# Expert gates fetched with the tokens, and the first expert layer's 64-channel parts paired on row halves

## What is computed

```python
xn2 = _layernorm(x, norm2_w, norm2_b).reshape(-1, C)         # 1152 x 192
logits = xn2 @ w_gate                                        # 8 experts
top_vals, top_idx = jax.lax.top_k(logits, 2)
gates = jax.nn.softmax(top_vals, axis=-1)
gates_full = zeros((T, E)).at[arange(T)[:, None], top_idx].add(gates)
# for every expert (w1 192x768, w2 768x192), with its column g of gates_full:
h = jax.nn.gelu(xn2 @ w1 + bb1, approximate=False)
acc = acc + g[:, None] * (h @ w2 + bb2)
return x + acc
```

## Time and profile before

| | us |
|---|---|
| median of 3 runs | 381.36 (380.62 to 381.72) |
| the profiled execution's own time | 382.74 |
| its span in the profile | 380.7 |
| PE busy / PEld / DVE / ACT / POOL | 319.8 / 285.3 / 229.8 / 167.8 / 83.5 |
| routing begins (DVE L1097) | 252.16 |
| first scatter issued | 282.62 |
| last scatter issued | 375.18 |

### The profile page before, as it was taken

The page is one execution under the profiler, slowest core; times in us unless marked ns, Lnnn a source line. Parts: engine busy times, 40 slices in busy tenths (PEclk is TensorE's granted clock), DMA queues, the critical chain, the costliest instruction groups (busy, mean ns, idle before and its releaser), DMA issues.

```text
span 380.7 us, 6780 instructions
## 1 busy us (share of the span) xinstructions
PE 319.8 (84%) x2358; PEld 285.3 (75%) x2358; DVE 229.8 (60%) x557; ACT 167.8 (44%) x399; POOL 83.5 (22%) x79
## 2 busy tenths in 40 slices
PE   7959740870597998999999989887999999999990
PEld 4948630560477787897898767786899999999990
DVE  1626999999998965416468478787333333333330
ACT  0053610524441519778796988314333333333320
POOL 9310002001000011101001000102225455556532
PEclk9989985796598999999999999997599999999997
DMA  7970000000000019691383133040102222222322
GB/s 262 317 223 3 0 0 0 0 2 0 1 2 1 0 46 282 196 270 55 106 245 86 37 85 125 25 116 13 43 10 38 38 45 41 44 43 42 47 29 23
DMA packets 20590, 28.01 MB, mean 74 GB/s; under 512 B 3459, under 2 KB 15475, under 8 KB 20555
## 3 DMA queue, kind: packets, MB, share of 16 engines
q1 hardware_dynamic: 16666, 23.52, 20.8%
q0 software_dynamic: 3888, 4.03, 7.2%
HBM read 22.77 MB, written 4.77 MB: 72 GB/s over the span
## 4 chain that ended last, share of the span: by engine, by line
PE 58%; DVE 22%; DMA 6%; ACT 5%; issue 5%; POOL 1%; POOLq 1%; SPq 0%; DVEq 0%; ACTq 0%
PE banks L1222 9%; PE banks L1223 8%; PE banks L1454 8%; PE banks L1301 7%; PE banks L1441 6%; PE banks L1443 6%; DMA out<-s,ffn 4%; PE banks L1252 3%; PE banks L1264 2%; ACT patch L770 2%; DMA patch<-in_xp 2%; PE banks L1345 2%; PE banks L1357 2%; DVE xh L922 2%; PE banks L1328 2%
## 5 line engine op out<-in xcount | busy, mean ns | idle before, releaser
L600 POOL TENSOR_TENSOR rs<-va,consts 96x6 f32<-96x6 f32 (+1 forms) x16 | 18.3, 1142 | 216.6 <-DVE va L900 120.1
L839 ACT ACTIVATE ffn<-banks 128x384 f32<-128x384 f32 x40 | 19.7, 492 | 61.3 <-PE banks L1443 56.6
L621 POOL DMA_INDIRECT out<-s,ffn x20 | 33.2, 1660 | 49.0 <-DVE s L1183 25.6
L1454 PE MATMUL banks<-arena,ffn 128*128 x240 | 42.1, 326 | 0.0
L1264 PE MATMUL banks<-consts,xh 96*128 96x96 f32 (+1 forms) x96 | 12.5, 273 | 32.1 <-DVEq L924 30.7
L1454 PEld LDWEIGHTS banks<-arena,ffn 128*128 128x128 f32 x240 | 38.5, 190 | 0.0
L1264 PEld LDWEIGHTS banks<-consts,xh 96*128 96x128 f32 (+1 forms) x96 | 9.8, 140 | 35.4 <-issue 32.6
L1183 DVE SCALAR_TENSOR_TENSOR s<-banks,ffn,ot 128x192 f32<-128x192 f32 x20 | 8.3, 417 | 33.1 <-PE banks L1454 33.0
L1301 PE MATMUL banks<-rvw,ffn 128*96 128x192 f32 x144 | 26.5, 336 | 1.0 <-ACT ffn L742 1.0
L611 POOL DMA_INDIRECT vs<-xh_scratch,ffn x21 | 21.1, 1004 | 26.6 <-DVE ffn L1143 17.3
L1252 PEld LDWEIGHTS banks<-arena,patch 128*96 128x96 f32 x144 | 24.1, 168 | 2.3 <-DMA patch<-in_xp 1.0
(11 more groups left out here) (210 smaller groups left out, 744.8 us busy)
## 6 DMA issues: line engine op xcount, KB each, us to landing
arena<-in_w SPq DMA_DIRECT2D x8, 576.0 KB, 9.0
patch<-in_xp SPq DMA_DIRECT2D x12, 288.0 KB, 6.1
arena<-in_w1a SPq DMA_DIRECT2D x8, 384.0 KB, 7.6
vs<-v_scratch SPq DMA_DIRECT2D x24, 114.8 KB
arena<-in_w1b SPq DMA_DIRECT2D x8, 195.0 KB
v_scratch<-vt SPq DMA_DIRECT2D x4, 229.5 KB, 3.0
xh_scratch<-xh SPq DMA_DIRECT2D x4, 216.0 KB, 2.3
out<-h SPq DMA_DIRECT2D x1, 864.0 KB
```

The costliest lines, as they stand in the source:

```text
L621: pool.indirect_dma_start(out[:, :], bass.IndirectOffsetOnAxis(ap=IS[:, j:j + 1], axis=0), YG[j % 2], None, compute_op=ALU.add).then_inc(s ...
L839: freed(A(HST[j % 2][:, 384 * i:384 * (i + 1)], ps[:, 0:384], ACT.Gelu), job)
L1454: ins = mm(ps[:, 0:C], HST[j % 2][:, 128 * k:128 * (k + 1)], W2[:, bass.ds(e, 1), C * k:C * (k + 1)], start=(k == 0), stop=(k == HB - 1))
```

## The change

The gates are no longer brought to their slots by matmuls. ACT takes tanh(d/2) of the two logits' difference (softmax of two is 0.5 +- 0.5 tanh), POOL makes a dense row of 8 gates per token (`GF`) with five instructions, and SP stores it behind the token's channels in `xh_scratch`, whose rows grow from 192 to 264 floats: 192 channels, the last 64 once more, 8 gates. The gather fetches all of it, and DVE takes a tile's gate column out of `XG` (`take_gate`). The "gates" matmuls and `RG` are gone. The expert's 64-channel weights now stand as two halves, blocks 0 to 2 on partitions 0 to 63 and blocks 3 to 5 on 64 to 127, against the doubled channels of the tokens; b1 is a bias of the gelu instead of a row of the matmul, which makes six gelu instructions of one block out of two of three. b1 is loaded as rows and turned by PE once (job "b1").

```diff
-FILL = "logits:2=3 turn:g:3=5 logits:3=3 rank=6 list=14"
+FILL = "logits:2=3 turn:g:3=5 logits:3=3 rank=6 list=14 xt:0=5"
-    out = [("rank",), ("list",), ("gates",)]
+    out = [("b1",), ("rank",), ("list",)]
 # SP
-                    load("w1b", W1B[0:C1 + 1, e, :], w1b[:, e, :])
+                    for r in range(2):
+                        load("w1b", W1B[C1 * r:C1 * (r + 1), e, :], w1b[0:C1, e, HID // 2 * r:HID // 2 * (r + 1)])
+                if n_experts < E and upto == E:
+                    load("b1", B1ROWS, w1b[C1, :, :].rearrange("e (m p) -> (e m) p", p=128))
+                    sp.dma_start(rows[:, :, 0:C], xh).then_inc(xh_stored[g], 16)
+                    sp.dma_start(rows[:, :, C:256], xh[:, :, 128:C]).then_inc(xh_stored[g], 16)
+            sp.wait_ge(gates_ready, 1)
+            sp.dma_start(xh_dram[:, 256:XW].rearrange("(t p) e -> p t e", p=T), GF).then_inc(gates_stored, 16)
             sp.wait_ge(h_done, TILES)
             sp.dma_start(out[0:TOK, :]...
 # POOL
+            pool.wait_ge(share_ready, 1)
+            pool.wait_ge(mask_ready, 1)
+            ch.then(pool.tensor_scalar(TG[:, 0:TILES], DD[:, 0:TILES], -0.5, 0.5, ALU.mult, ALU.add))
+            ch.then(pool.tensor_scalar(TG[:, TILES:NC2], DD[:, 0:TILES], 0.5, 0.5, ALU.mult, ALU.add))
+            ch.settle()
+            for c, part in enumerate((G1, G2)):
+                ch.then(pool.tensor_tensor(part, MK[:, c], bc(TG...), ALU.mult))
+            ch.settle()
+            pool.tensor_tensor(GF.rearrange("p t e -> p e t"), G1, G2, ALU.add).then_inc(gates_ready, 1)
             pool.wait_ge(list_ready, 1)
+            pool.wait_ge(gates_stored, 16)
             def gather(j):
                 if j >= 3:
                     full(pool, ("xt", j - 3))
+                    pool.wait_ge(gate_taken, j - 2)
 # ACT
-            A(DD[:, 0:TILES], DD[:, 0:TILES], ACT.Exp).then_inc(e2_ready, 1)
+            A(DD[:, 0:TILES], DD[:, 0:TILES], ACT.Tanh, scale=0.5).then_inc(share_ready, 1)
-                    freed(A(HST[j % 2][:, 384 * i:384 * (i + 1)], ps[:, 0:384], ACT.Gelu), job)
+                    for m in range(3 * i, 3 * i + 3):
+                        ins = A(HST[j % 2][:, 128 * m:128 * (m + 1)], ps[:, 128 * (m % 3):128 * (m % 3 + 1)], ACT.Gelu, bias=WE[j % 2][:, ...])
+                    freed(ins, job)
             for j in range(1, FULL):
-                gelu(j)
                 if j + 1 < MT:
                     turned(j + 1)
+                gelu(j)
 # DVE, weights(j)
-                ch.then(CP(we[:, 0:1, :], W1A[:, bass.ds(e, 1), :]))
-                ch.step(CP(we[0:C1 + 1, 1:2, :], W1B[0:C1 + 1, bass.ds(e, 1), :]))
+                ch.then(CP(we[:, 0:HID].unsqueeze(1), W1A[:, bass.ds(e, 1), :]))
+                ch.then(CP(we[:, HID:h1].unsqueeze(1), W1B[:, bass.ds(e, 1), :]))
+                if j >= 2:
+                    taken(dve, ("h", j - 2, 1))
+                ch.step(CP(we[:, h1:h1 + HB].unsqueeze(1), B1[:, bass.ds(e, 1), :]))
+            def take_gate(j):
+                dve.wait_ge(gathered[j % 3], 16 * (j // 3 + 1))
+                e = dve.value_load(EJI[0:1, j:j + 1], min_val=0, max_val=E - 1)
+                CP(LST[:, MT + j:MT + j + 1], XG[j % 3][:, 256:XW][:, bass.ds(e, 1)]).then_inc(gate_taken, 1)
             for j in range(FULL):
+                if j + 2 <= FULL:
+                    take_gate(j + 2)
                 gated(j)
 # PE
+            ps = begin(("b1",))
+            end(pe.transpose(ps[:, 0:E * HB], B1ROWS, ident[0:E * HB, 0:E * HB]), ("b1",))
-            ps = begin(("gates",))        ... 48 matmuls
+                ps = [begin(("h", j, i)) for i in range(2)]
+                for m in range(HB):
+                    mm(ps[m // 3][:, ...], we[:, 128 * m:128 * (m + 1)], xt[:, 0, :], start=(m % 3 == 0), stop=False)
+                for k in range(3):
+                    for i in range(2):
+                        r = slice(C1 * i, C1 * (i + 1))
+                        ins = mm(ps[i][:, 128 * k:128 * (k + 1)], we[r, HID + 128 * k:HID + 128 * (k + 1)], xt[r, 1, :], start=False, stop=(k == 2))
```

More of the change, by code:

```diff
@@ L272, in build @@
         names = ["chan", "const", "tokw", "tokb", "kvrw", "wow", "kfw", "rfw", "vfw", "qkvw", "projw",
-                 "gatew", "b2", "w1a", "w1b", "w2"]
+                 "gatew", "b2", "w1a", "w1b", "b1", "w2"]
         loaded = {n: sem("loaded_" + n) for n in names}
@@ L421, in build @@
         ONEB = rcarve(NC2 * 64).rearrange("p (i b) -> p i b", b=64)
-        RT, RG, AA = (rcarve(NC2 * 2 * MT).rearrange("p (i a) -> p i a", a=2 * MT) for _ in range(3))
+        RT, AA = (rcarve(NC2 * 2 * MT).rearrange("p (i a) -> p i a", a=2 * MT) for _ in range(2))
         qat = {"q": 0, "k": 0}
@@ L438, in build @@
         EJ = qcarve(MT, "k")[0:T]
+        GF = rcarve(TILES * E).rearrange("p (t e) -> p t e", e=E)
+        G1, G2 = (qcarve(TILES * E, "k")[0:T].rearrange("p (e t) -> p e t", e=E) for _ in range(2))
         assert MT <= 32 and 128 * 9 >= TOK
@@ L447, in fcarve @@
             return ffn[:, fat[0] - n:fat[0]]
-        XG = [vs_[:, C * i:C * (i + 1)] for i in range(3)]
+        XG = [vs_[:, XW * i:XW * (i + 1)] for i in range(3)]
         YG = [S[:, i, 0:C] for i in range(2)]
@@ L457, in build @@
         GB = OT[:, 0, 0, 0:C]
-        WE = [x.rearrange("p (b n) -> p b n", b=2) for x in (rvw[:, :], fcarve(2 * HID))]
+        WE = [rvw[:, 0:HID + HID // 2 + HB], fcarve(HID + HID // 2 + HB)]
         v_dram = nc.dram_tensor("v_scratch", [TOK, NH * HW], F32).ap()
-        xh_dram = nc.dram_tensor("xh_scratch", [TOK, C], F32).ap()
+        xh_dram = nc.dram_tensor("xh_scratch", [TOK, XW], F32).ap()
         block = ctx.enter_context(nc.Block())
@@ L601, in _ @@
                     nstat += 1
+            pool.wait_ge(share_ready, 1)
[4 more added lines that the diff above has]
+            for c, part in enumerate((G1, G2)):
+                ch.then(pool.tensor_tensor(part, MK[:, c], bc(TG[:, TILES * c:TILES * (c + 1)].unsqueeze(1), [T, E, TILES]), ALU.mult))
+            ch.settle()
+            pool.tensor_tensor(GF.rearrange("p t e -> p e t"), G1, G2, ALU.add).then_inc(gates_ready, 1)
             pool.wait_ge(list_ready, 1)
+            pool.wait_ge(gates_stored, 16)
             for g in range(G):
-                pool.wait_ge(xh_stored[g], 16)
+                pool.wait_ge(xh_stored[g], 32)
             def gather(j):
@@ L1105, in _ @@
             TTR(DD[:, 0:TILES], TOP[:, :, 1], TOP[:, :, 0], ALU.subtract).then_inc(top_ready, 1)
+            ps = full(dve, ("b1",))
+            freed(CP(B1.rearrange("p e m -> p (e m)"), ps[:, 0:E * HB]), ("b1",))
+            taken(dve, ("b1",))
             ps = full(dve, ("rank",))
@@ L1136, in weights @@
                 we = WE[j % 2]
-                ch.then(CP(we[:, 0:1, :], W1A[:, bass.ds(e, 1), :]))
-                ch.step(CP(we[0:C1 + 1, 1:2, :], W1B[0:C1 + 1, bass.ds(e, 1), :]))
-                dve.sem_inc(we_ready, 1)
+                h1 = HID + HID // 2
+                ch.then(CP(we[:, 0:HID].unsqueeze(1), W1A[:, bass.ds(e, 1), :]))
[3 more added lines that the diff above has]
+                ch.step(CP(we[:, h1:h1 + HB].unsqueeze(1), B1[:, bass.ds(e, 1), :]))
+                dve.sem_inc(we_ready, 1)
+            ch.step(TTR(EJC[:, :, :], bc(slot[:, 0:MT].unsqueeze(2), [T, MT, E]), bc(END[:, 0:E].unsqueeze(1), [T, MT, E]), ALU.is_ge))
+            ch.step(RED(EJ[:, :], EJC[:, :, :], AX.X, ALU.add))
+            ch.step(TS(EJI[0:T, :], EJ[:, :], float(E - 1), None, ALU.min))
+            ch.then(TS(USED[0:T, :], END[:, E - 1:E], 1.0 / 128, None, ALU.mult))
+            ch.then(dve.memset(O[:, 0, :], 0.0))
             ps = full(dve, ("list",))
@@ L1144, in _ @@
             freed(CP(LST[:, 0:MT], ps[:, 0:MT]), ("list",))
[L1145 to L1162, removed]
             taken(dve, ("list",))
@@ L1166, in _ @@
             dve.sem_inc(index_ready, 1)
+            full(dve, ("rv", TILES - 1))
+            dve.wait_ge(loaded["w1a"], 16 * E)
+            dve.wait_ge(loaded["w1b"], 32 * E)
+            weights(0)
             weights(1)
-            ps = full(dve, ("gates",))
-            freed(CP(LST[:, MT:2 * MT], ps[:, 0:MT]), ("gates",))
-            taken(dve, ("gates",))
+            def take_gate(j):
+                dve.wait_ge(gathered[j % 3], 16 * (j // 3 + 1))
+                e = dve.value_load(EJI[0:1, j:j + 1], min_val=0, max_val=E - 1)
+                CP(LST[:, MT + j:MT + j + 1], XG[j % 3][:, 256:XW][:, bass.ds(e, 1)]).then_inc(gate_taken, 1)
+            for j in range(2):
+                take_gate(j)
             dve.wait_ge(loaded["b2"], 16)
@@ L1193, in rest @@
                         for j in pair(a):
+                            if j + 1 < MT:
+                                take_gate(j + 1)
                             gated(j)
@@ L1408, in _ @@
             end(ins, ("list",))
[L1410 to L1419, removed]
+            for n, k in (("w1a", 1), ("w1b", 2), ("w2", 1)):
```

(13 more changed lines are left out.)

23 lines of the change are left out of this document (16 added, 7 removed).

## The result

The changed kernel takes **376.65 us** (median of 4 runs, 375.78 to 378.16) against 381.54 for the kernel before in the same comparison: the ratio of the times is 0.9881, its 95% interval 0.9854 to 0.9908. It is 4.9 us faster, where 10.1 were forecast. The profiled execution took 376.50, its span 374.7.

A forecast was written before the change was run, and what follows sets the result against it. PE was taken to bound the kernel, at 4.85 us a tile hardly above the scatters' own pace. Head -3.9 and loop -6.2 make -10.1 from 381.36: 371.2 us, range 366.0 to 378.3.

The forecast's parts named there:

- Head: Up to the first scatter: without the gates matmuls it comes at 278.7 instead of 282.62, 3.9 us less.
- the bound of 6.0: Good end for the stretch up to the first scatter: high clock from the start, 6.0 us less.
- Gate row: POOL's five instructions 3 us, SP's store 3, in DRAM at 260.5 ahead of the gathers: priced at nothing, 2 in range.
- PE's tile: PE in the loop: 4.85 us less 0.61 for overlapping pairs plus 0.18 for two mode changes, 4.42 a tile.
- A change of mode that costs a matmul's whole latency: PE in the loop, by the Trainium skill's rule: some 0.27 us a change, tile 4.78; the forecast took 0.09.
- The rival in which weight loads bind: PE's loop: loads of a pair go one after the other, nothing saved, mode changes added: 382.4 us; chance 0.08.
- my 0.61 for the overlap: The 64-channel matmuls of up: twelve records in 0.73 us instead of 1.34, 0.61 less a tile.
- DVE ... 3.8 of 4.42 ... All hidden: DVE's work in the loop, 3.8 us a tile, stays below PE's 4.42, so it does not bind.
- two setbacks: Scatters in the loop: 84.0 us at PE's pace plus 2.4 for two meetings with instruction fetches, 86.4.
- scatters bind with every fetch: Rival for the loop: 4.80 us a tile whatever PE does, 91.2 for the steps, 376.1 in all; chance 0.25.
- at 0.45 I had bounded them: ACT in the loop: six gelus at 0.45 us each and two copies take 3.6 at most, below PE's 4.42.

The follow-up runs named there:

- take_next: The changed kernel with DVE taking the gate of tile j+1 ahead of result j instead of that of tile j+2: 372.0 us, ratio 0.9765.
- bare_wait: take_next with DVE again waiting for the gather of tile j+2 at the head of each turn, copying nothing from it: 377.23 us.
- four_buffers: The changed kernel with four buffers of gathered tokens instead of three, each gather issued one scatter earlier, DVE's order unchanged: 371.02 us, ratio 0.973.

## Why the prediction was right and wrong

- **Head: right in kind, too small.** Forecast 3.9 us less at the first scatter, measured 5.75. The first gather came 0.4 earlier. Up(0) started at 268.8 (forecast 269.1), so the gather's landing was well sized. The rest is the clock, whose return I put at 274, with an earlier return as the bound of 6.0; it was back at 266.7 in this execution. The 5.5 us from which I had 274 took the transposes for the start of dense work, though PE was busy without a gap in the 5.33 us of "gates" matmuls before them as well, also at half clock; so 274 had no good ground.
- **Gate row: right.** POOL's five instructions took 1.64 us from 252.64 (3 were taken), and the first gather waited for the list, not for the row.
- **PE's tile: nearly right.** Forecast 4.42, measured 4.53 (4.52 for the tile from 273.95 to 278.47 in the changed kernel, before the ring holds it up): the pairs with their mode changes and the transposes beside them cost 0.11 more. A change of mode that costs a matmul's whole latency, a tile of 4.78, did not come: the entry took 0.09. The rival in which weight loads bind is out: pairs overlapped. But my 0.61 for the overlap compared it with 65-row matmuls at 0.112 a record. Against 64-row matmuls without overlap it is 0.32.
- **The step that failed: "DVE ... 3.8 of 4.42 ... All hidden".** I counted DVE's work per tile and found it below PE's. I did not ask when its turn may begin. `take_gate(j + 2)` stands ahead of everything in it and waits for a gather that is queued behind a scatter and lands 4.7 us after that scatter's issue (346.07 to 350.78). From there DVE needs 4.6 to the scatter of the result. A throughput of 3.8 (the sum counts the result's 0.4 twice, but a turn that waited for no gather, 307.10 to 311.13, did take 4.03) was about right and didn't matter; the latency around the ring is 9.3 for two tiles, and more with a late gather. take_next, bare_wait and four_buffers show it from three sides.
- **Scatters.** I expected 86.4 us for 19 steps from PE's pace and two setbacks. With the ring opened it is 87.9 and 88.1, 1.5 to 1.7 too few, about what PE's 0.11 a tile comes to (2.1). The rival "scatters bind with every fetch" gives 376.1, close to what was measured, but by luck: take_next has the same scatters and fetches and takes 4.63 a step.
- **What the gap is made of.** The changed kernel's profile is 1.8 us better than forecast up to the first scatter and 5.9 worse in the loop (92.31 for 86.4). The wait is 4.4 of these 5.9 (92.31 less take_next's 87.93), PE's tile the rest. That take_next's 372.0 lies so near the forecast of 371.2 is partly luck: its head is 2.5 better than forecast, its loop 1.5 worse. That the change's 376.65 lies inside the range of 366.0 to 378.3 is no credit to the mechanism either, which gave 6.2 us to a loop that won 0.25.
- **Sums.** In the rival of the weight loads, 3.1 less 0.4 plus some clock is at least 2.7, not about 2; and with 2 for the head and 3.0 from 19 tiles at two changes of 0.09 it is slower already at 0.09 and turns at 0.05. Neither bears on the forecast.

## What to carry to other kernels

When an instruction with a wait is put at the head of an engine's turn, busy time per turn is not enough: follow the event waited for back to what issued it, and if that leads to the engine's own earlier results, add up the ring and divide by the turns that it spans. A wait that is free beside a slow engine becomes the bound once that engine is made faster, so one edit of a change can hide what another is worth; time each with the other's obstacle removed. The remedy is small: take the value one turn later, or, for one more buffer, issue the fetch one turn earlier.

## What was not expected of the hardware

- Six 64-row float32 matmuls, three on one half of the rows, then three on the other, took 1.19 us, mode change included, where six of 65 rows took 1.34 without any; only 0.32 was left for the overlap to win (0.87).
- Going from 128-row to 64-row matmuls cost little: L1472's twelve records took 1.43 to the first of L1477 (310.90 to 312.33), 0.09 over 1.34, as the entry into the column pairs of the earlier trace rows had it.
- Six gelus of 128 columns cost 1.65 us together, 0.28 each, with 0.39 shown for one in the groups of instructions; at 0.45 I had bounded them well above that.
- A scatter that only writes lands in 2.4 us in the median, one that adds in 3.6, and issuing it holds POOL 0.99 us instead of 1.59.
